# Route logits from 16 fp16 products and a fold, k rotated before the route on GpSimd, and xn's transposes placed inside the first output projection

## What is computed

```python
x = x + tanh(g_xattn) * wkv(time_decay, time_first, layernorm(x), ctx_2048)
```

```python
h = silu(xn_prev * conv_w[:, 0] + xn * conv_w[:, 1])     # _prev: the batch before
q, k, v, g = silu(h @ Wq), h @ Wk, h @ Wv, h @ Wg        # 16 heads, rotary on q and k
logits = einsum('bhld,hdr->bhlr', v, router_w)           # 2 routes per head
# softmax, argmax: only tokens of the same route see each other; q is scaled
# by the route's probability and by 1 / (tokens of that route so far)
o = causal_linear_attention(q, k, v)                     # then normalised per head
out = (silu(g) * o) @ Wout
x = x + tanh(g_ffn) * out
```

## Time and profile before

| What | us |
|---|---|
| median of three runs | 1753.68 |
| the profiled execution: its own time | 1754.45 |
| the profiled execution: span, first to last instruction | 1752.7 |
| TensorE (PE) busy | 1624.3 |
| VectorE (DVE) busy | 1465.3 |
| ScalarE (ACT) busy | 741.6 |
| GpSimd (POOL) busy | 612.2 |

### The profile page before, as it was taken

How to read it: one execution, slowest core, us unless ns; L and a number is a source line. 1 busy time by engine, 2 the same in 40 slices (tenths; PEclk the granted TensorE clock), 3 DMA queues, 4 the chain that set the end, 5 groups by cost and what they waited for, 6 DMA issues and landing times.

```text
span 1752.7 us, 37624 instructions
## 1 busy us (share of the span) xinstructions
PE 1624.3 (93%) x15799; PEld 866.7 (49%) x15799; DVE 1465.3 (84%) x2004; ACT 741.6 (42%) x933; POOL 612.2 (35%) x716
## 2 busy tenths in 40 slices
PE   0445999999999999999999999999999999999996
PEld 0123555555555555555555555555555555555552
DVE  7898988888889888888898888888888888889832
ACT  4835344344443443444434434444344444443420
POOL 1421433443223434432234344322343444223321
PEclk9867999999999999999999999999999999999998
DMA  9500011111100111111111111110001111100000
GB/s 269 191 13 25 5 33 37 37 38 38 28 25 30 29 37 37 37 38 29 27 30 28 37 37 38 37 35 24 30 25 37 38 37 38 37 25 26 14 13 25
DMA packets 23416, 70.77 MB, mean 40 GB/s; under 512 B 2256, under 2 KB 2512, under 8 KB 23248
## 3 DMA queue, kind: packets, MB, share of 16 engines
q1 hardware_dynamic: 23248, 68.37, 13.6%
HBM read 51.59 MB, written 16.78 MB: 39 GB/s over the span
## 4 chain that ended last, share of the span: by engine, by line
PE 88%; DVE 8%; issue 2%; ACT 1%; POOL 1%; DMA 0%; SPq 0%; POOLq 0%; DVEq 0%; ACTq 0%
PE ps_g L383 25%; PE ps_g L384 24%; PE ps_g L387 24%; PE ps_o L535 4%; PE ps_t L478 3%; PE ps_t L375 3%; PE ps_o L375 2%; DVE big L775 2%; PE ps_t L520 1%; PE ps_s L520 1%; DVE seg L823 1%; DVE big L792 0%; PE ps_s L497 0%; DVE seg L814 0%; DMA small<-in_g_ffn 0%
## 5 line engine op out<-in xcount | busy, mean ns | idle before, releaser
L383 PE MATMUL ps_g<-big,h_hi 128*128 128x512 f16 x1536 | 585.5, 381 | 3.2 <-DVE h_lo L996 3.2
L384 PE MATMUL ps_g<-big,h_hi 128*128 128x512 f16 x1536 | 585.4, 381 | 0.0
L387 PE MATMUL ps_g<-big,h_lo 128*128 128x512 f16 x1536 | 584.9, 381 | 0.0
L387 PEld LDWEIGHTS ps_g<-big,h_lo 128*128 128x128 f16 x1536 | 150.7, 98 | 183.8 <-issue 4.2
L1149 POOL TENSOR_TENSOR small<-small 128x1 f32<-128x1 f32 x64 | 14.2, 221 | 648.8 <-DVE small L808 648.6
L383 PEld LDWEIGHTS ps_g<-big,h_hi 128*128 128x128 f16 x1536 | 158.7, 103 | 165.0 <-issue 7.3
L384 PEld LDWEIGHTS ps_g<-big,h_hi 128*128 128x128 f16 x1536 | 150.7, 98 | 165.3 <-issue 3.4
L383 PE MATMUL ps_g<-big 128*128 128x512 f16 x512 | 195.3, 382 | 0.7 <-DVE big L884 0.7
L384 PE MATMUL ps_g<-big 128*128 128x512 f16 x512 | 194.8, 380 | 0.0
L387 PE MATMUL ps_g<-big 128*128 128x512 f16 x512 | 194.7, 380 | 0.0
L1168 POOL TENSOR_TENSOR vx<-vx,ek 128x1024 f32<-128x1024 f32 x32 | 75.3, 2353 | 337.0 <-ACT ek L607 326.1
(11 more groups left out here) (158 smaller groups left out, 2902.5 us busy)
## 6 DMA issues: line engine op xcount, KB each, us to landing
x_ring<-in_x SPq DMA_DIRECT2D x32, 512.0 KB
vx<-in_ctx SPq DMA_DIRECT2D x32, 512.0 KB
out<-x_ring SPq DMA_DIRECT2D x32, 512.0 KB
big<-in_wv SPq DMA_DIRECT2D x2, 2048.0 KB, 21.1
big<-in_wg SPq DMA_DIRECT2D x2, 2048.0 KB, 20.7
big<-in_wout SPq DMA_DIRECT2D x2, 2048.0 KB, 20.1
big<-in_wq SPq DMA_DIRECT2D x1, 2048.0 KB, 14.5
big<-in_wk SPq DMA_DIRECT2D x1, 2048.0 KB, 20.1
```

Source lines behind the costliest of these rows:

```text
L383: nc.tensor.matmul(dst[:, :], hi, hi_of(u)[:, kc * HALF:(kc + 1) * HALF], start=(kc == 0), stop=False)
L384: nc.tensor.matmul(dst[:, :], hi, lo_of(u)[:, kc * HALF:(kc + 1) * HALF], start=False, stop=False)
L387: last = nc.tensor.matmul(dst[:, :], lo, hi_of(u)[:, kc * HALF:(kc + 1) * HALF], start=False, stop=(kc == KC - 1))
```

## The change

**Route logits.** w_route is scaled by a bound and split in fp16 high and low parts that lie side by side, 32 columns for each of the 8 chunks (`w_route_hl`). 16 fp16 products take these as stationary parts (128x32) and h_hi, then h_lo, as moving parts (128x128); chunk kc writes to the 32 PSUM partitions of kc modulo 4, so that the four strips each hold a partial sum of (high, low) x 16 heads, transposed. ScalarE copies that 128x128 block (`copy_logits`), and one fp32 matmul (`route_logits`, the fold) with the 128x16 matrix r_sum sums the strips and parts per head, undoes the scale and turns the result back. The products read h_hi and h_lo and no longer fa.

**Order on TensorE.** The products stand after the gate's maximum, between q and k; the fold after k; sign sums after v0 and no longer before it. xn's transposes stand between the two halves of o0 and no longer behind it.

**Order elsewhere.** VectorE's signs move from between the denominator's terms and its scan to behind the rotation of q. ScalarE's route_prob moves behind the copy of k. GpSimd rotates k first and then makes the route matrix. The wait of the denominator's terms for the logits is gone.

**Opening.** VectorE takes the maximum of the router's difference (r_max) once, and `split_route_weights` makes the scales, r_sum and the split after the last route chunk.

The diff, without declarations of scratch columns and semaphores:

```diff
@@ -125,6 +125,8 @@
         turn = work[:, 3 * C + HALF:4 * C]
         to_batch = turn[:, 0:P]
         w_route = turn[:, P:2 * P]
+        w_route_hl = turn[:, 2 * P:3 * P].bitcast(F16)
+        logits_t = turn[:, 3 * P:4 * P]
         q_sb = work[:, 4 * C:4 * C + HALF]
         k_sb = work[:, 4 * C + HALF:5 * C]
         rot_q = work[:, 5 * C:5 * C + HALF]
...
@@ -397,8 +402,6 @@
             def step(i, slot, main, nxt, nxt2, prev, prev2):
                 n, p = i + 1, i - 1
                 if main:
-                    if not opening(i):
-                        route_logits(i)
                     unit_ready(i, UQ)
                     bank_free(i, 0, prev2)
                     after(pe, s_hlo, 2 * i + 1)
@@ -408,18 +411,21 @@
                 if prev:
                     gate_max_turn(p)
                 if main:
+                    if not opening(i):
+                        route_products(i)
                     unit_ready(i, UK)
                     bank_free(i, 1, prev2)
                     project(ps_g[1], h_hi, h_lo, UK, s_kp)
                     if opening(i):
                         for r in range(5, 9):
                             bound_row(r)
-                        pe.wait_ge(s_wroute, 8)
-                        route_logits(i)
-                    sign_sums(i)
+                        pe.wait_ge(s_rw, 8)
+                        route_products(i)
+                    route_logits(i)
                     unit_ready(i, UV)
                     after(pe, s_q, i + 1)
                     project(ps_g[0], h_hi, h_lo, UV, s_vp)
+                    sign_sums(i)
                     after(pe, s_rq, i + 1)
                     transposes(ps_t[0], rot_q, s_qtp, as_is)
                     unit_ready(i, UV + 1)
@@ -459,8 +465,8 @@
                                 after(pe, s_gtlo, 2 * p + part + 1)
                             project(ps_g[g], gt_hi, gt_lo, UO + g, s_up, part,
                                     (lambda: values_ready(i, g)) if main and part else None)
-                        if g == 0 and nxt:
-                            xn_transposes(n, main)
+                            if g == 0 and part == 0 and nxt:
+                                xn_transposes(n, main)
                         if main:
                             values(i, g)
 
@@ -471,13 +477,21 @@
                 else:
                     after(pe, s_sg, 2 * (i - 1) + g + 1)
 
+            def route_products(i):
+
+                after(pe, s_hlo, 2 * (i + 1))
+                for a in (h_hi, h_lo):
+                    for kc in range(KC):
+                        rows = slice(kc % 4 * 2 * H, (kc % 4 + 1) * 2 * H)
+                        last = nc.tensor.matmul(ps_t[1][rows, 0:P], w_route_hl[:, kc * 2 * H:(kc + 1) * 2 * H],
+                                                a[:, kc * P:(kc + 1) * P], start=(a is h_hi and kc < 4),
+                                                stop=(a is h_lo and kc >= 4))
+                last.then_inc(s_dlp, 1)
+
             def route_logits(i):
 
-                after(pe, s_h, i + 1)
-                for kc in range(KC):
-                    last = nc.tensor.matmul(ps_t[1][:, 0:H], fa[:, kc * P:(kc + 1) * P], w_route[:, kc * H:(kc + 1) * H],
-                                            start=(kc == 0), stop=(kc == KC - 1))
-                last.then_inc(s_dl, 1)
+                after(pe, s_dlc, i + 1)
+                nc.tensor.matmul(ps_t[1][:, P:P + H], logits_t, r_sum, start=True, stop=True).then_inc(s_dl, 1)
 
             def gate_max_turn(p):
                 after(pe, s_gm2, p + 1)
@@ -633,11 +647,12 @@
                     after(act, s_sp, i)
                     A(q_sb, ps_g[0][:, :], ACT.Silu, scale=inv[:, UQ:UQ + 1]).then_inc(s_q, 1)
                     if not opening(i):
-                        route_prob(i)
+                        copy_logits(i)
                     act.wait_ge(s_kp, i + 1)
                     A(k_sb, ps_g[1][:, :], ACT.Copy, scale=inv[:, UK:UK + 1]).then_inc(s_k, 1)
                     if opening(i):
-                        route_prob(i)
+                        copy_logits(i)
+                    route_prob(i)
                 if nxt:
                     seed(n)
                 if main:
@@ -675,10 +690,15 @@
                 if nxt2:
                     exp_k(i + 2, (slot + 2) % 4)
 
+            def copy_logits(i):
+                act.wait_ge(s_dlp, i + 1)
+                after(act, s_dl, i)
+                A(logits_t, ps_t[1][:, 0:P], ACT.Copy).then_inc(s_dlc, 1)
+
             def route_prob(i):
                 act.wait_ge(s_sgp, i + 1)
                 after(act, s_cf, i)
-                A(pr, ps_t[1][:, 0:H], ACT.Abs).then_inc(s_th, 1)
+                A(pr, ps_t[1][:, P:P + H], ACT.Abs).then_inc(s_th, 1)
                 act.wait_ge(s_th, 2 * i + 1)
                 A(pr, pr, ACT.Tanh, scale=0.5).then_inc(s_th, 1)
 
@@ -783,6 +803,30 @@
                                 routed[m % 2].rearrange("p (k h d) -> p k h d", k=2, d=DV), AX_X, ALU.add)\
                  .then_inc(s_wroute, 1)
 
+            def split_route_weights():
+
+                V.tensor_reduce(r_sum, ident[:, :].rearrange("p (j h) -> p h j", h=H), AX_X, ALU.add).then_inc(s_rw, 1)
+                dve.wait_ge(s_rw, 2)
+                dve.wait_ge(s_wsc, UV + 2)
+                V.tensor_scalar(r_bound, r_max, mx[:, UV:UV + 1], mx[:, UV + 1:UV + 2], ALU.mult, ALU.max).then_inc(s_rw, 1)
+                dve.wait_ge(s_rw, 3)
+                V.tensor_scalar(r_bound, r_bound, TINY, None, ALU.max).then_inc(s_rw, 1)
+                dve.wait_ge(s_rw, 4)
+                V.reciprocal(r_scale, r_bound).then_inc(s_rw, 1)
+                dve.wait_ge(s_rw, 5)
+                V.tensor_scalar(r_scale, r_scale, W_TOP, None, ALU.mult).then_inc(s_rw, 1)
+                V.tensor_scalar(r_inv, r_bound, mx[:, U:U + 1], LN_BOUND / (W_TOP * H_TOP), ALU.mult, ALU.mult)\
+                 .then_inc(s_rw, 1)
+                dve.wait_ge(s_rw, 7)
+                dve.wait_ge(s_wroute, 8)
+                hl = w_route_hl.rearrange("p (k s h) -> p k s h", s=2, h=H)
+                rows = w_route.rearrange("p (k h) -> p k h", h=H)
+                V.tensor_scalar(r_sum, r_sum, r_inv, None, ALU.mult).then_inc(s_rws, 1)
+                V.tensor_scalar(hl[:, :, 0, :], rows, r_scale, None, ALU.mult).then_inc(s_rws, 1)
+                dve.wait_ge(s_rws, 2)
+                V.scalar_tensor_tensor(hl[:, :, 1, :], rows, r_scale, hl[:, :, 0, :], ALU.mult, ALU.subtract)\
+                 .then_inc(s_rw, 1)
+
             def centre(u):
 
                 m = u - UV
@@ -841,9 +885,6 @@
                     V.tensor_reduce(ossq, by_head(squares, DV), AX_X, ALU.add).then_inc(s_ss, 1)
                 if nxt:
                     denominator_terms(n)
-                if main:
-                    signs(i)
-                if nxt:
                     denominator_scan(n)
                 if prev:
                     out_scale(p)
@@ -851,6 +892,7 @@
                     dve.wait_ge(s_q, i + 1)
                     after(dve, s_op, 2 * i)
                     rotate(dve, V, i, 0, q_sb, rot_q, s_r1q, s_rq)
+                    signs(i)
                     if opening(i):
                         lo_unit(4)
                 if nxt:
@@ -903,7 +945,7 @@
                 dve.wait_ge(s_dl, i + 1)
                 after(dve, s_route, i)
                 after(dve, s_cump, i)
-                V.tensor_scalar(sgn, ps_t[1][:, 0:H], 0.0, 2.0, ALU.is_ge, ALU.mult).then_inc(s_sgp, 1)
+                V.tensor_scalar(sgn, ps_t[1][:, P:P + H], 0.0, 2.0, ALU.is_ge, ALU.mult).then_inc(s_sgp, 1)
                 dve.wait_ge(s_sgp, i + 1)
                 V.tensor_scalar(sgn, sgn, -1.0, None, ALU.add).then_inc(s_sgn, 1)
 
@@ -938,7 +980,6 @@
                 dve.wait_ge(s_e, 2 * (n + 1))
                 after(dve, s_hlo, 2 * n)
                 after(dve, s_pre, n)
-                after(dve, s_dl, n)
                 recurrence_terms(n, ek[:, :], carry_b, s_sva, s_ekt, fa[:, :], s_fda)
 
             def denominator_scan(n):
@@ -1104,6 +1145,8 @@
             dve.wait_ge(s_router, 16 * 6)
             V.tensor_tensor(x_ring[:, 2, :], x_ring[:, 2, :], x_ring[:, 3, :], ALU.subtract).then_inc(s_base, 1)
             tokens_by_time()
+            dve.wait_ge(s_base, 1)
+            V.tensor_reduce(r_max, x_ring[:, 2, :], AX_X, ALU.max, apply_absolute_value=True).then_inc(s_rw, 1)
             lo_unit(0)
             conv_products(0, 0)
             conv_products(0, 1)
@@ -1121,6 +1164,7 @@
             centre(UV)
             for m in range(4, 8):
                 route_chunk(m)
+            split_route_weights()
             centre(UV + 1)
             spread(5, 4)
             spread(6, 5)
@@ -1206,14 +1250,14 @@
                     G.tensor_tensor(by_head(sg, DV), by_head(sg, DV), per_head(fac, 0, H, DV), ALU.mult)\
                      .then_inc(s_sgf, 1)
                 if main:
```

(6 more changed lines are left out.)

7 lines of the change are left out of this document (5 added, 2 removed).

## The result

The changed kernel takes 1723.22 us (median; 1723.12 to 1723.76) against 1753.97 us (1753.19 to 1754.88) for the kernel before, timed beside it: a ratio of 0.9823, 95% interval 0.981 to 0.9835. The prediction was 1732, range 1722 to 1752. The profiled execution took 1723.12 us, its span 1721.3 us.

The account below looks back on a forecast made before the run. The prediction took the loop to be bound by TensorE's instruction stream, with VectorE close behind and bounding the opening. Terms: 1754.45 + 5.3 (opening) - 30 x 0.96 (steps) + 0.84 (last step) = 1731.8, so 1732 us; range 1722 to 1752.

Parts of the forecast that it names:

- The products: TensorE, after Q: 16 fp16 products that replace 1.80 us of fp32 logits take 0.7 us, range 0.45 to 1.9.
- B: Rival on TensorE: products don't overlap with their weight loads and take 1.1 to 1.6 us; 1744 to 1758 us; chance 0.12.
- E: Rival on TensorE: products take 1.8 us, with mode changes on top, so no TensorE gain; 1766 us; chance 0.03.
- The step: TensorE's step: 49.93 - 1.80 + 0.70 + 0.14 = 48.97 us, 0.96 less.
- Fold, copy, h_lo: Waits added to TensorE by h_lo, ScalarE's copy and the fold: nothing; the fold itself takes 0.14 us.
- The opening: Before step 1's Q, VectorE bound: router maximum, scales and route_prob ahead of the seed make Q 5.3 us later.
- Cover of the sign sums: TensorE reaches sign sums 16.4 us after Q starts, VectorE's signs end 12.7 after: cover 3.7 us, no wait.
- xn's transposes: TensorE: moving them ahead by 12 matmuls, 2.6 us, brings no time of its own and buys slack.
- The replay: VectorE and GpSimd queues replayed with collisions: squares' sum to numerator's end 20.7 us, VectorE's chain stays at 48.2 us.
- C: Rival: VectorE becomes the bound, chain 49.0 to 49.6 us, still faster; 1734 to 1751 us; chance 0.10.
- D: Rival, slower: GpSimd's k rotation and route collide with VectorE's numerator; at +2.3 us, step 50.6, 1781 us; chance 0.07.

Follow-up runs that it names:

- e4: Changed kernel with the 16 fp16 products issued twice: 1729.98 us, ratio 0.986 to the kernel before.
- e5: Changed kernel with all 16 products on one 32-column strip and the fold over those 32 rows alone: 1752.60 us, ratio 0.999 to the kernel before.
- e6: Changed kernel with ScalarE's route_prob, in the first step alone, behind the seed and the split of unit 4: 1719.97 us, ratio 0.98 to the kernel before.
- e10: Changed kernel with the sign sums put back ahead of v0 on TensorE: 1799.78 us, ratio 1.0262 to the kernel before.
- e1: Changed kernel with xn's transposes put back behind the second half of o0: 1758.29 us, ratio 1.0021 to the kernel before.
- e3: Kernel before with only xn's transposes moved between the halves of o0: 1753.72 us, ratio 0.9995 to the kernel before.
- e12: e1 with the sign sums moved between the halves of v1: 1758.37 us, ratio 1.0019 to the kernel before.
- e11: Changed kernel with one unused VectorE maximum of 1024 values between the recurrence's output and its transpose: 1732.97 us, ratio 0.9876 to the kernel before.
- e8: Changed kernel with two unused VectorE maxima of 1024 values behind the signs: 1737.87 us, ratio 0.9904 to the kernel before.
- e9: e1 with GpSimd making the route before it rotates k: 1764.65 us, ratio 1.0059 to the kernel before.
- e7: Changed kernel with one unused VectorE maximum of 1024 values behind the signs: 1723.64 us, ratio 0.9822 to the kernel before.

## Why the prediction was right, and where it was off

**What bounds the kernel.** TensorE's stream, and its full effect in the time: right; e4 shows it one for one.

**The products: the term that was mis-sized.** I took 0.7 us from a range of 0.45 to 1.9, allowing 0.1 on each side for the mode and 0.45 for the stream. Measured: 0.40 us in all, 0.22 of it the products (e4), so they are just outside the lower end, and the forecast of a step was 0.30 us too long by this term. The lower bound doubled the values' 0.016 us for twice the columns; e4 and e5 show that four strips stream 128 columns in 0.0575 us side by side, 0.014 us each, less than the values' instructions with half the columns. The rivals in which products do not overlap (B, E) are excluded. The rule of the Trainium skill (TensorE: Matmul & The Clock Gate, Part 3, The mechanism), that a load overlaps only where its row group differs, gave an estimate of 83 ns each. The trace disagrees: 14 ns over four strips, and 57.5 ns on one strip, where every load uses all rows and the same columns as the matmul before it.

**The step.** 49.93 - 1.80 + 0.40 + 0.14 = 48.67; measured 48.73, predicted 48.97. The measured time, 1723.22, lies close to the lower end of the range, 1722. Over the 30 intervals the gain was 36.6 us where I had 28.8, 7.8 of the 8.7 us by which the forecast was too high. The rest is the last step: I added 0.84 for its products and fold, and behind Q of step 31 the changed kernel is in fact 0.05 us shorter (profiled times). The products and fold are there: the last transposes of the gated output start 57.38 us behind that Q (1699.90), against 56.76 before (1730.56), 0.62 more. What takes them back is luck: TensorE waits 9.1 us ahead of these transposes in both kernels and then runs at a granted clock of 0.50, and in the last output projection the clock comes back sooner in the changed kernel (0.88 of full over the first 9.48 us, against 0.81).

**Fold, copy, h_lo: nothing but the fold's 0.14.** Right: TensorE has no wait there.

**The opening.** Right in size and by its steps: signs(0) at 127.4 (127.3 predicted), seed done at 130.2, the low parts done at 136.9, Q of step 1 at 178.32 (178.3). The wait that I named, route_prob ahead of the seed, was undone in e6; I expected about what it gave back.

**Cover of the sign sums.** Predicted 3.7 us: TensorE there 16.4 us after Q starts, signs 12.7 after. Measured: TensorE at 830.26, 16.25 after Q (814.01), signs done at 827.29, 13.3 after; cover 3.0. The cover is V's 5.2 us (without it, e10, TensorE waits 2.1 to 2.2), and the whole of it goes once xn is late (e1).

**xn's transposes: the step that failed.** I wrote that the move brings no time of its own and buys slack, and took the 1.61 us that VectorE waited for xn as VectorE's distance to the bound, 48.3 us against 49.93. e3 bears out the first half. The second was wrong: that wait is a part of the loop and not slack in it. The transposes are late because TensorE's queue holds them behind same_route, and same_route is held by VectorE's read of the sums; the loop had 0.1 us left. Without the move the new logits gain nothing (e1, e12), so it is a condition of the whole gain. That the forecast for the full change came out is in this part luck: both moves were in it, but it gave no reason why they had to be.

**VectorE and GpSimd.** The replay had the numerator's end 20.7 us after the squares' sum; measured 20.4 (814.78 to 835.17), q's rotation 3.7 us (under 4.5 said), the collisions moved to scan and route as it had them. VectorE's chain, forecast at 48.2 us a step, is 47.96 without its waits for TensorE, and its slack of 0.8 is 0.77 (e11); the loop through same_route, which the prediction did not have, has 0.94. Rivals C and D did not come about in the changed kernel. C's mechanism is real: in e8 and e11 the step grows once the slack is gone. D's was not seen in any run. The collision with the numerator came about in e9, but GpSimd bore it and its rotated k was late; VectorE read the sums 19.9 us after the squares' sum, sooner than in e1 (21.1). The place of the signs that the prediction gave as no cost is none only because V and the early xn leave them 3.0 us of cover.

**What stays open.** No run lets VectorE read the sums sooner, or gives same_route another bank, with xn late; that their loop sets the step rests on the waits of e1 and e12 and on what xn's move did. Why the step is 0.06 us longer than its terms, and which of e8's two step lengths (49.0 mostly, 49.9 at times) is set by what, was not followed up.

## What to carry to other kernels

A wait of a second engine is slack only if the loop that it closes does not run through the bound engine's own queue: add the pieces of each loop (transposes to sum, sum to read, read to the instruction that reuses the bank, and back to the transposes) before you shorten the bound engine, and look for an instruction that starts within 0.1 or 0.2 us of its release though no wait is shown. The pieces of every closed chain add up to the step, so look also for waits inside them: only the loop without any is the bound. If one loop has 0.1 us left, shortening the bound engine by 1.2 us gains no more than that until something in that loop is moved. And one experiment that removes a wait does not prove that it was the only one: the next may stand right behind it, as e12 showed.

## What the hardware showed that I had not expected

- At the full granted clock, small fp16 matmuls (stationary 128x32, 128 moving columns) that turn over four column strips cost 0.014 us each and on one strip 0.0575 us; entering and leaving costs some 0.18 us for the set (0.40 - 0.22).
- An fp32 product over 32 rows between full-size ones costs about 0.4 us (e5: 1086.01 to 1086.33, with 0.09 ahead of it), the same over 128 rows 0.14 (824.94 to 825.08).
- When both are in two-input operations, GpSimd and VectorE hold each other up on both sides: the route took 1.05 us with VectorE idle (changed kernel's opening, 127.63) and 3.16 beside the scan, the scan 2.42 and 3.37; GpSimd's sin products 1.45 and, beside the numerator, 4.52. Short operations are caught too: the signs' second one took 0.17 us where GpSimd stood still (e9, 1095.98) and 1.04 beside its rotation (826.25). So the 1.21 us of work added to VectorE cost 0.4 us of its chain where GpSimd was busy beside it (e7) and 1.04 where GpSimd was idle (e11).
